# Attention stage of a fused layer on one core: nine slots per pair of sequences instead of ten, normalised tokens turned in between, normalisation applied by GpSimd, two of eight turned heads copied by ScalarE

## What is computed

```python
h = concatenate([s4d(x), txt], axis=1)                    # (16, 205, 1024)
n = layernorm(h)                                          # (h - mean) / sqrt(var + 1e-5)
q = (n @ Wqkv)[..., :1024] as 32 heads of 32; k, v = next 32, last 32 columns, shared by all heads
scores = where(pos_k <= pos_q, q k^T * 32**-0.5 + slope[head] * (pos_k - pos_q), -1e30)
h = h + (softmax(scores) @ v) @ Wo
h = h + base(layernorm(h)) + routed LoRA of 8 experts(layernorm(h))
```

## Time and profile before

| | us |
|---|---|
| median of 3 runs | 1736.79 (1732.65 to 1740.34) |
| the profiled execution's own time | 1738.08 |
| its span, first to last instruction | 1736.3 |
| PE busy / PEld busy | 1507.8 (87%) / 1335.7 (77%) |
| DVE busy | 1134.3 (65%) |
| ACT busy | 737.2 (42%) |
| POOL busy | 536.6 (31%) |

### The profile page before, as it was taken

How to read it: one execution, slowest core, us unless ns; L and a number is a source line. 1 busy time by engine, 2 the same in 40 slices (tenths; PEclk the granted TensorE clock), 3 DMA queues, 4 the chain that set the end, 5 groups by cost and what they waited for, 6 DMA issues and landing times. The chain is left out here.

```text
span 1736.3 us, 31628 instructions
## 1 busy us (share of the span) xinstructions
PE 1507.8 (87%) x9700; PEld 1335.7 (77%) x9700; DVE 1134.3 (65%) x4142; ACT 737.2 (42%) x2624; POOL 536.6 (31%) x314
## 2 busy tenths in 40 slices
PE   0355399989999999999999769999999999999999
PEld 0355288878878787887888558888988888888887
DVE  7999378879788878879787854443444434344343
ACT  3455157777767767767878631011000010100100
POOL 1788314443534343443445400110101111010110
PEclk9877689999999999989999679999999999999999
DMA  6144455454554445445455341212112121211201
GB/s 200 37 89 93 103 98 109 80 83 96 80 103 73 104 72 108 73 75 100 79 117 88 103 171 47 73 37 72 48 60 72 36 72 40 69 66 43 73 32 40
DMA packets 110527, 139.63 MB, mean 80 GB/s; under 512 B 13156, under 2 KB 96484, under 8 KB 110040
## 3 DMA queue, kind: packets, MB, share of 16 engines
q1 hardware_dynamic: 110408, 138.41, 34.8%
HBM read 62.82 MB, written 40.30 MB: 59 GB/s over the span
## 5 line engine op out<-in xcount | busy, mean ns | idle before, releaser
L700 ACT ACTIVATE P<-P,nmax 128x128 f32<-128x128 f32 (+1 forms) x1024 | 434.3, 426 | 95.1 <-DVE nmax L790 88.9
L764 POOL TENSOR_TENSOR P<-P,rden 128x512 f32<-128x512 f32 (+1 forms) x256 | 329.2, 1308 | 451.5 <-DVE rden L796 451.4
L790 DVE CUSTOM_DVE_ANT_0 P<-sc,mask 128x128 f32<-128x128 f32 (+1 forms) x1024 | 292.4, 323 | 101.1 <-PE sc L612 94.7
L1126 POOL TENSOR_TENSOR h<-h,base_b 128x1024 f32<-128x1024 f32 (+1 forms) x26 | 84.2, 3240 | 637.4 <-DVE xn L1153 637.4
L642 PE MATMUL pr<-xT_hi,wq_hi 128*128 128x410 f32 x576 | 243.0, 422 | 0.0
L802 DVE COPY PTR<-pt 128x282 f32<-128x282 f32 x512 | 222.2, 435 | 30.3 <-PE pt L622 17.1
L1039 PE MATMUL b<-w_hi,x2T_hi 128*128 128x390 f32 (+3 forms) x624 | 214.8, 344 | 14.3 <-DVE h L1199 13.2
L1039 PE MATMUL b<-w_lo,x2T_hi 128*128 128x390 f32 (+3 forms) x624 | 212.4, 340 | 0.0
L1039 PE MATMUL b<-w_hi,x2T_lo 128*128 128x390 f32 (+3 forms) x624 | 212.0, 340 | 0.0
L642 PE MATMUL pr<-xT_lo,wq_hi 128*128 128x410 f32 x576 | 204.0, 354 | 0.0
L642 PE MATMUL pr<-xT_hi,wq_lo 128*128 128x410 f32 x576 | 202.9, 352 | 0.0
(11 more groups left out here) (174 smaller groups left out, 3049.1 us busy)
## 6 DMA issues: line engine op xcount, KB each, us to landing
Qs<-q_hi SPq DMA_DIRECT2D x128, 205.0 KB, 4.5
Qs<-q_lo SPq DMA_DIRECT2D x64, 205.0 KB, 5.5
att_dram<-att SPq DMA_DIRECT2D x64, 205.0 KB, 2.4
at<-att_dram SPq DMA_DIRECT2D x25, 512.0 KB, 4.6
h<-h_dram SPq DMA_DIRECT2D x25, 512.0 KB, 3.4
out<-h SPq DMA_DIRECT2D x25, 512.0 KB, 2.6
h_dram<-Y SPq DMA_DIRECT2D x64, 128.0 KB, 3.0
ht<-h_dram SPq DMA_DIRECT2D x16, 512.0 KB, 5.8
```

Of the source, the lines that this page charges most:

```text
L700: last = nc.scalar.activation(P[rows, j % 2, i, cols], P[rows, j % 2, i, cols], ACT.Exp, scale=-1.0, bias=nmax[at], accum_out=den[at])
L764: lastp = nc.gpsimd.tensor_tensor(w, w, r, ALU.mult)
L790: lastv = v.tensor_tensor_reduce(P[0:n, j % 2, i, cols], sc[i % 2][0:n, cols], mask[0:n, m], 1.0, 3.0e38, ALU.add, ALU.min, nmax[0:n, j % ...
L1126: nc.gpsimd.tensor_tensor(h2[0:n, par, :], h2[0:n, par, :], base_b[0:n, :], ALU.add).then_inc(biased, 1)
```

## The change

- `SLOTS` is 9. The slot of its own for turning the tokens is gone; `MAIN` holds the nine projections, with keys and values fourth and query blocks 3 to 7 behind them. `SCORE_SLOT` is 5 to 12 without a gap, so of nine slots only slot 4 has no scores.
- The tokens are turned in chunks of 128 features over all four token tiles (four transposes each, `turn_ln`), at the places `LN_AT`: steps 0, 1, 3, 4 and 6 of slot 8 for the next pair, steps 0, 2 and 4 of its slot 0. ScalarE writes the high part one step later (`hi_ln`), VectorE the low part two steps later (`lo_ln`). For pair 0 all eight stand ahead of slot 0.
- Projections use banks 0 and 1 in turn and bank 2 in slot 8; chunks use bank 0 for the first and third and bank 1 for the others, and a chunk waits until the one before it in its bank has been read.
- The next pair's tokens are loaded once all eight chunks are turned, statistics start at step 14, and GpSimd applies the normalisation, two tiles in slot 5 and two in slot 6, ahead of its half units there.
- ScalarE copies turned heads 3 and 7 of each unit (`ACT_TURNS`), VectorE the other six.

```diff
-SLOTS = 10
+SLOTS = 9
...
-    MAIN = ["ln", ("q", 0), ("q", 1), "kv", ("q", 2), ("q", 3), ("q", 4), ("q", 5), ("q", 6), ("q", 7)]
-    USE = {0: 8, 1: 9, 2: 11, 3: 12, 4: 14, 5: 15, 6: 16, 7: 17}
-    KV_USE, VT_USE = 10, 13
+    MAIN = [("q", 0), ("q", 1), ("q", 2), "kv", ("q", 3), ("q", 4), ("q", 5), ("q", 6), ("q", 7)]
...
+
+    MAIN_BANK = [0, 1, 0, 1, 0, 1, 0, 1, 2]
+    VT_BANK = 2
     V_SLOT = 6
-    LN_HI_AFTER, LN_LO_AFTER = 1, 2
-    SCORE_SLOT = [5, 6, 7, 8, 9, 11, 12, 13]
-
...
+    LN_SLOT = SLOTS - 1
+    APPLY_SLOTS = [5, 6]
+    LN_AT, LN_BANK, FIRST_BANK = [0, 1, 3, 4, 6, 8, 10, 12], [0, 1, 0, 1, 1, 1, 1, 1], [i % BANKS for i in range(KC)]
...
+    def ln_chunk(slot, i, after):
+
+        at = (slot - LN_SLOT) % SLOTS * GH + i - after
+        return LN_AT.index(at) if at in LN_AT else None
...
+    def ln_pair(p, slot, first, last):
+
+        if slot == LN_SLOT:
+            return p + 1 if last is False else None
+        return p if not first and last is not None else None
...
+        return max(i for i in range(KC) if banks[i] == bank)
+    ACT_TURNS = [3, 7]
...
+    SCORE_SLOT = [5, 6, 7, 8, 9, 10, 11, 12]
...
+                    if slot == 1 and last is False:
+                        sp.wait_ge(ln_turned, KC * p + KC)
+                        for s in range(4):
+                            load_h(p + 1, s)
...
-                    if slot == 1 and last is False:
-                        for s in range(4):
-                            sp.wait_ge(proj_done, BANK_USES * p + 4 + s + 1)
-                            load_h(p + 1, s)
...
+                if i >= 2:
+                    wait_turned(pe, p, j, i - 2)
+                elif not isinstance(p, int) or p + j > 0:
+                    wait_turned(pe, *((p, j - 1) if j else (p - 1, UNITS - 1)), i + GH - 2)
...
+            def turn_ln(p, i):
+
+                banks = banks_of(p)
+                if i == 0:
+                    pe.wait_ge(xn_ready, 4 * p + 4)
+                if banks[i] in banks[:i]:
+                    pe.wait_ge(ln_read, KC * p + max(k for k in range(i) if banks[k] == banks[i]) + 1)
+                else:
+                    wait_count(pe, main_read, SLOTS * p - 2 + banks[i])
+                for s, (c, t0, n) in enumerate(TILES):
+                    at = c * S + t0
+                    last = nc.tensor.transpose(pr[banks[i]][:, at:at + n], ht[0:n, s, i * 128:(i + 1) * 128], ident[0:n, 0:n])
+                last.then_inc(ln_turned, 1)
+
...
             def main_step(p, slot, what, i):
-                if what == "ln":
-                    wait_count(pe, bank_read, BANK_USES * p + i - BANKS + 1)
-                    s, half = i % 4, i // 4
-                    if half == 0:
-                        pe.wait_ge(xn_ready, 4 * p + s + 1)
-                    n = TILES[s][2]
-                    for q in range(4):
-                        last = nc.tensor.transpose(pr[i % BANKS][:, 128 * q:128 * q + n],
-                                                   ht[0:n, s, (4 * half + q) * 128:(4 * half + q + 1) * 128], ident[0:n, 0:n])
-                    last.then_inc(proj_done, 1)
-                    return
...
-                if i == KC // 2 and what == ("q", 0):
-                    pe.wait_ge(bank_read, BANK_USES * p + 8)
...
+                    if slot == 0:
+                        pe.wait_ge(ln_read, KC * p + last_in(banks_of(p), 0) + 1)
+                    elif slot == 1:
+                        pe.wait_ge(ln_read, KC * p + KC)
+                    elif slot == SLOTS - 1:
+                        pe.wait_ge(vt_read, p + 1)
+                    else:
+                        pe.wait_ge(main_read, SLOTS * p + slot - 1)
+                if slot == 0 and i > last_in(banks_of(p), 0):
+                    pe.wait_ge(ln_read, KC * p + i + 1)
...
+                        chunk, pair = ln_chunk(slot, i, 0), ln_pair(p, slot, first, last)
+                        if chunk is not None and pair is not None:
+                            turn_ln(pair, chunk)
...
+            def hi_ln(p, i):
+                act.wait_ge(ln_turned, KC * p + i + 1)
+                nc.scalar.activation(xT[0][:, i, :], pr[banks_of(p)[i]][:, 0:PT], ACT.Copy).then_inc(ln_hi, 1)
...
+            def copy_turned(p, j, i):
+                act.wait_ge(transposed, 64 * p + 8 * j + i + 1)
+                if i == ACT_TURNS[0]:
+                    wait_count(act, av_done, 8 * p + j - 1)
+                nc.scalar.activation(PTR[:, j % 2, i, :], pt[i % 2][:, 0:S + TXT], ACT.Copy).then_inc(pT_act, 1)
...
-                        turn = GH * slot + i - LN_HI_AFTER
-                        if 0 <= turn < GH and main is not None:
-                            hi_part(p, 0, turn)
...
+                        chunk, pair = ln_chunk(slot, i, 1), ln_pair(p, slot, first, last)
+                        if chunk is not None and pair is not None:
+                            hi_ln(pair, chunk)
...
+                        turning = tj if i >= 4 else aj
+                        if turning is not None and (i + 4) % GH in ACT_TURNS:
+                            copy_turned(*turning, (i + 4) % GH)
...
+            def ln_apply(p, s):
+                n = TILES[s][2]
+                if s == 0:
+                    wait_apart(pool, rstd_ready, p + 1, rows_ready, 3)
+                nc.gpsimd.tensor_scalar(ht[0:n, s, :], ht[0:n, s, :], mv[0:n, s, 0:1], rstd[0:n, s:s + 1],
+                                        ALU.subtract, ALU.mult).then_inc(xn_ready, 1)
...
+                        if half == 0 and last is False and slot in APPLY_SLOTS:
+                            for s in range(2):
+                                ln_apply(p + 1, 2 * APPLY_SLOTS.index(slot) + s)
...
-        STATS_AT, RSTD_RATE = 12, 1
-        APPLY_AT, APPLY_EVERY = 36, 1
-        CHAINS = 8 + 4 + 1 + RSQRT_LINKS
+        STATS_AT, RSTD_RATE = 14, 1
...
+            def lo_ln(p, i):
+                dve.wait_ge(ln_hi, KC * p + i + 1)
+                v.tensor_tensor(xT[1][:, i, :], pr[banks_of(p)[i]][:, 0:PT], xT[0][:, i, :].bitcast(F32), ALU.subtract).then_inc(ln_read, 1)
...
+            def ln_apply(s):
                 n = TILES[s][2]
                 if s == 0:
-                    link.wait()
+                    dve.wait_ge(rstd_ready, 1)
                 v.tensor_scalar(ht[0:n, s, :], ht[0:n, s, :], mv[0:n, s, 0:1], rstd[0:n, s:s + 1],
...
+                        chunk, pair = ln_chunk(slot, i, 2), ln_pair(p, slot, first, last)
+                        if chunk is not None and pair is not None:
+                            lo_ln(pair, chunk)
...
-                            for s in range(4):
-                                if turn == APPLY_AT + APPLY_EVERY * s:
-                                    ln_apply(p + 1, s, link)
                         turning = tj if i >= 4 else aj
-                        if turning is not None:
+                        if turning is not None and (i + 4) % GH not in ACT_TURNS:
```

More of the change, by code:

```diff
@@ L41 @@
 PT = 2 * S
-SLOTS = 10
+SLOTS = 9
 BANKS = 3
-BANK_USES = 18
 GH = 8
@@ L471, in attention_block, with banks_of, last_in, wait_turned @@
     STACKS = 3
[L473 to L481 removed]
+    MAIN = [("q", 0), ("q", 1), ("q", 2), "kv", ("q", 3), ("q", 4), ("q", 5), ("q", 6), ("q", 7)]
+    Q_SLOT = [MAIN.index(("q", k)) for k in range(KC)]
+    KV_SLOT = MAIN.index("kv")
+    MAIN_BANK = [0, 1, 0, 1, 0, 1, 0, 1, 2]
+    VT_BANK = 2
+    V_SLOT = 6
+    LN_SLOT = SLOTS - 1
[8 more added lines that the diff above has]
+        return p if not first and last is not None else None
+    def banks_of(p):
+        return FIRST_BANK if isinstance(p, int) and p == 0 else LN_BANK
+    def last_in(banks, bank):
+        return max(i for i in range(KC) if banks[i] == bank)
+    ACT_TURNS = [3, 7]
+    def wait_turned(eng, p, j, i):
+        by_act = sum(k <= i for k in ACT_TURNS)
+        if i in ACT_TURNS or i == GH - 1:
+            wait_count(eng, pT_act, len(ACT_TURNS) * (8 * p + j) + by_act)
+        if i not in ACT_TURNS or i == GH - 1:
+            wait_count(eng, pT_copied, (GH - len(ACT_TURNS)) * (8 * p + j) + i + 1 - by_act)
+    SCORE_SLOT = [5, 6, 7, 8, 9, 10, 11, 12]
     def att_unit(slot, lag):
@@ L559, in body @@
                 for slot, main, sj, tj, aj in slots(p, first, last):
+                    if slot == 1 and last is False:
+                        sp.wait_ge(ln_turned, KC * p + KC)
+                        for s in range(4):
+                            load_h(p + 1, s)
+                    if slot == 1 and last is True:
+                        sp.wait_ge(ln_turned, KC * p + KC)
+                        for k in range(4):
+                            load_wo(k)
                     if last is None and slot == 1:
@@ L572, in body @@
                         load_wo(8)
-                    if slot == 1 and last is True:
-                        for k in range(4):
-                            sp.wait_ge(proj_done, BANK_USES * p + 4 + k + 1)
-                            load_wo(k)
```

(28 more changed lines are left out.)

97 lines of the change are left out of this document (40 added, 57 removed).

## The result

The changed kernel takes **1776.78 us** (median of 4, 1775.68 to 1783.15) against 1735.43 (4 runs, 1732.65 to 1740.34): ratio 1.0235, 95% interval 1.021 to 1.026. It is slower by 41 us where 1703 and "faster" stood, and outside the range of 1682 to 1732. The profiled execution is the slowest of the four (1783.15), so its trace shows some 45 us more where the medians show 41.

A forecast was written before the change was run, and what follows sets the result against it. TensorE was taken as nearest the bound, with 84.2 us of work in pairs of 97.1, so only waits could be gained. Attention's stretches summed to 751.4 against 786.4, 35.0 less than before: 1703 us, range 1682 to 1732.

The forecast's parts named there:

- jumps: Slot 0 of pairs 2 to 6: jump back stays at 3.1 us each, five times, bounds 2.2 and 4.
- turned heads: ScalarE's copies of heads 3 and 7 just fit TensorE's path; 0.5 us a pair, between 0 and 7.
- clock: Loop pairs: 1.2 us a pair left for the slow clock, of some 3, after taking 1.8 off.
- what it credited to the copies on ScalarE: Behind pair 7, 11 copies leaving VectorE save 4.8 us; slot 2 has six VectorE copies, not eight.
- The applies: Normalisation on GpSimd, slots 5 and 6: 1.1 us each, priced by a one-input cast, adding nothing to the time.
- The limit of 1.6 us each: Slot 6: two applies between GpSimd's half units cost nothing if each takes under 1.6 us.
- the rival: Applies at the two-input price, 3.3 us, make unit 1's turns 3.4 late; 24 in seven pairs, 1727; chance 0.10.
- the rival in which the copies gate TensorE throughout: ScalarE's turned-head copies come late; at 0.45 us per copy 7.2 a pair, 1761 in all; chance 0.10.
- Statistics: VectorE's statistics in slots 1 to 3: 1.0 us in slot 2 and 0.2 in slot 3, 1.2 a pair.
- TensorE's work of a pair: Matmuls and transposes of one pair take TensorE 84.2 us, the same before and after the change.
- the wait for Qs: Start of slot 7: scores' 2.16 us wait for query block 3's last transfer goes, saving 2.2 a pair.
- The named signs of a wrong forecast: TensorE idle before turns behind ScalarE's copy, full slots above 10 us, applies over 1.6, a loop pair above 95.

The follow-up runs named there:

- e5: The changed kernel with applications on VectorE, all turned heads copied by VectorE and pairs 1 to 6 written out instead of looped; 1689.2 us.
- e10: The changed kernel with all applications on VectorE and all eight turned heads copied by VectorE, loop kept; 1722.6 us.
- e1: The changed kernel with all four applications of a pair back on VectorE, the rest as changed; 1736.1 us.
- e7: The changed kernel with 96 small memsets ahead on VectorE, shifting its code in the instruction stream; 1780.9 us, one run.
- e8: The changed kernel with 192 small memsets ahead on VectorE, shifting its code in the instruction stream; 1780.1 us, one run.
- e11: The changed kernel with pairs 1 to 6 written out on VectorE alone, the other engines keeping the loop; 1770.6 us.

## Why the prediction was wrong

The runs lead from e5 to the changed kernel one step at a time, so the measured steps add up to the error of 73.8 us (1776.8 - 1703) by construction; each is good to some 3 us. The forecast for e5's form is 1703 less its terms for jumps (5 x 3.1), turned heads (7 x 0.5) and clock (6 x 1.2), which is 1676.8, and plus what it credited to the copies on ScalarE: 4.8 us in the rest and two copies of VectorE less in slot 2 (2 x 0.435, seven pairs, 6.1), together 1687.7.

| step | forecast | measured | missed |
|---|---|---|---|
| nine slots, chunks, statistics (e5) | 1687.7 | 1689.2 | 1.5 |
| jump back and its clock (e5 to e10) | 22.7 | 33.4 | 10.7 |
| copies on ScalarE (e10 to e1) | -7.4 | 13.5 | 20.9 |
| applications on GpSimd (e1 to changed) | 0 | 40.7 | 40.7 |

- **The applies, the step that failed.** "It has one tensor input, so I take 1.1, by the first": the price is 3.78 us. The cast that I took it from the earlier trace rows is another operation, on 4 partitions, without per-partition scalars; which of these makes the price no run separates. The limit of 1.6 us each held (above), and the rival had the right mechanism, with a chance of 0.10 and a price too low on two counts: 3.3 for 3.78, and no slow clock behind the wait. Seven pairs pay 5.8 us each, about 4.3 of it the wait. The page cited ahead, "GPSIMD Engine Reference", section "Engine selection" of the Trainium skill, speaks against the move and was right in that; its near parity for one input is not what this trace shows, 3.78 us against 0.81.
- **The jump.** Taken unchanged at 3.1 with bounds of 2.2 and 4; it is 5.5 us in slot 0 of the changed kernel with its clock and 5.9 in e10, and 6.4 to 6.7 by the whole time. I carried the price over from a slot 0 whose first work was a turned head's copy. In the nine-slot form that first work is a chunk's low part that gates TensorE in every step, and VectorE's gap grew from about 2.5 to 4.4 us. Bounds on an unchanged mechanism have to be taken anew when what stands behind it changes. Written out, the kernel before saves 21 us, more than its 5 x 3.1: that much had been there all along.
- **Turned heads on ScalarE.** The credit for a VectorE with fewer copies didn't come: slot 2 takes 11.06 us in e10 and 11.10 in e1, with two copies less. A copy takes 0.385 us (0.42 taken), and the rival in which the copies gate TensorE throughout didn't come: 0.4 us in a full slot. The rest behind pair 7 is where it went wrong: I credited ScalarE's eleven copies with 4.8 us and overlooked the weight splits that stand in its queue there. 61.0 us measured, 54.3 forecast; with all copies on VectorE it is 53.7 to 55.0.
- **Statistics.** In the changed kernel slots 2 to 4 take 11.10, 10.68 and 9.00 us against 9.81, 9.65 and 8.70 in pair 7, which has none: 2.6 a pair, where 1.2 was taken. In e5, with all copies on VectorE, it is 3.5 (10.95, 10.51 and 9.09 against 9.46, 9.29 and 8.28), where the same count gives 2.1. Slots 3 and 4, where the statistics end and the root chain runs, take 1.3 and 2.0 together instead of 0.2, and that was the term costed too low. That the first row misses by only 1.5 is luck in part: e5's pairs are 1.5 us dearer than the 87.3 that the terms give for them (six pairs, 9 us), its rest 4.1 cheaper (55.0 for 59.1).
- **Right**: TensorE's work of a pair, 84.2 (e5's pair less 3.5 for the statistics is 85.3); the wait for Qs gone, slot 6 at 7.4; slot 8 at 12.0 to 12.5, with ScalarE at 10.56 of 12.4 us; a pair without a jump or a late GpSimd at 88.1 (e5: 88.8, near by offsetting terms, since the 88.1 holds 1.2 for a slow clock that e5 doesn't have); pair 7 at 83.7 (84.5).
- The named signs of a wrong forecast, applications over 1.6 us and a loop pair above 95, are both in the profile.

**Open.** Why VectorE's gap behind a jump grew by some 2 us. It is not the place in the stream (e7, e8), and mostly not GpSimd's or ScalarE's new work (e10, still 4.0 to 4.1). The traces have a candidate: before, the jump came where data took 23.4% of the DMA engines' time, now it comes where it takes 94.6%, and the transfers of instructions in the gap take 0.9 to 1.0 us where they took 0.31 to 0.68. No run separates this from the rest of the nine-slot body. It matters little for the sum, as e11 shows: ScalarE's gap alone keeps slot 0 at 15 to 16 us.
